# An attention kernel with image-prompt tokens: the hand-written order of its units is rearranged

## The chip, the cores and the metric

The kernel runs on one core of a Trainium2 chip. The metric is the device time of one execution in microseconds (us), lower is better. The engines are TensorE (PE in the rows; PEld is its weight load), VectorE (DVE), ScalarE (ACT), GpSimd (POOL) and SyncE (SP, which here only issues transfers).

## What is computed

Eight batches of cross attention with 20 heads of 16 channels. The context has 371 text tokens and 4 image-prompt tokens.

```python
q = heads(x @ W_q); k = heads(text @ W_k); v = heads(text @ W_v)
probs = softmax(q k^T * D**-0.5)                 # 112 x 371, 20 heads, 8 batches
text_out = probs @ v
k_ip, v_ip = heads(ip @ W_k_ip), heads(ip @ W_v_ip)
qsem = l2norm(probs @ text)                      # 112 x 512 for each head
sem  = qsem @ l2norm(ip)^T
p_ip = softmax(q k_ip^T * D**-0.5 + 0.5 * sem) * mask
out  = (text_out + p_ip @ v_ip) @ W_out + b_out + x
```

The norm of `probs @ text` is not formed from its 512 columns. It is e G e^T with the Gram matrix G = text text^T, of which only the upper blocks are used; that is why a diagonal block has to be halved and corrected before it can be multiplied.

## The kernel before

Every engine walks one list of units, `master_schedule()`, and issues what that unit means for it; a unit that means nothing to an engine is skipped. So the list sets the program order of all five queues at once, and semaphores do the rest. For VectorE the list is passed through `behind()` (line 142), which holds back a K, G or GV unit until after the next max, gram, mT or o.

A batch b is five rounds (groups of four heads), g = 5b + r. The words of a round stand in `ROUNDS` for batches 1 to 6, `EARLY` for batch 0, `LATE` for the last round of batches 5 and 6, `SECOND` and `NO_K` for the first round of batches 1 and 6, and `LAST` for batch 7. While batch b is worked on, batch n = b + 1 is prepared and batch b + 2 gets its keys. The words that matter here:

- `S0 S1 S2` (St): scores of round g + 1 in three blocks of keys. Four matmuls of 99 rows into P (line 1276), then two ScalarE passes, exp into `eb` and a rounded copy into `er` (lines 813, 817). S0 of a batch's first round waits for the rows of maxima, `s_mr` (line 1273).
- `g2 g1 g0` (gram, lines 1279 to 1295): Gram block column times `er`, 5, 3 and 1 matmuls into Y. VectorE multiplies the product by `eb` (line 1025), GpSimd adds the products of g1 and g0 (line 633).
- `v` (pv): values and row sums of the previous round into O (line 1309).
- `m` (max): scores of one head of batch n, without exp, and their row maximum on VectorE (line 1001). All 20 come before `mT`, which transposes them; SP then writes three rows into `qst` (line 519).
- `K0 K1 K2`: keys of batch b + 2, from `eh` and `el`, the rounded and the rest part of the context. `Kr`: SP loads them back in stacked form (lines 494 to 514).
- `E` (split): for batch b + 3, ScalarE makes the two halves of `eh` (line 739), then GpSimd the two halves of `el` (line 644).
- `C`, `G0 G1 GV V0 V1`: Gram blocks and values of batch n.
- `D`: VectorE's three steps on the diagonal blocks of n: `dl` (line 974), `lh` (line 978), and `Gh` times a triangle (line 980). `L`: a matmul with `dl` (line 1229) and VectorE's five steps after it (lines 989, 994, 997); the first g2 of batch n waits for the last, `s_wd` (line 1286).
- `p`, `pT`, `cT`, `o`: end of batch b - 1. ScalarE evicts pT into `pTs` (line 851); cT (lines 1343 to 1354) needs that and gives `cTh` on ScalarE and `cTl` on VectorE (line 1101); `o` is nine matmuls that need `cTl` (line 1391).
- `T0 T1 r0 r1 r2 pw z`: the small steps of batch b - 1's image-prompt softmax.

The units with results in the three banks `PR` share them in turn (`seq`, `NR`), so a unit waits until the third before it has been read.

Of the kernel before, what the change touches and what calls it, by code (L numbers as in the profile page):

```python
# [5 lines left out]
B, S, C, E = 8, 112, 320, 512  # L6
NTOK, NIP = 375, 4
T = NTOK - NIP
H, D = 20, 16
# [17 lines left out]
K0 = (len(STACK) + 6) * 16  # L27
# [9 lines left out]
def spread(core, *others):  # L37

    keyed = []
    for w, units in enumerate((core,) + others):  # L40
        keyed += [((k + 0.5) / len(units), w, u) for k, u in enumerate(units)]
    return [u for _, _, u in sorted(keyed, key=lambda t: (t[0], t[1]))]


def flat(units):
# [2 lines left out]

ROUNDS = ("K0 S0 m g2 m g1 S1 m K1 m S2 m g0 v G0",
# [4 lines left out]
SECOND = "S0 K0 m g2 g1 m S1 m g0 K1 m v S2 m G0"  # L56
NO_K = "m m S0 g2 m g1 v g0 S1 S2 m m G0"
EARLY = ("m S1- m S2- K1 S0 m g2 g1 S1 m m g0 m S2 K2",
# [4 lines left out]
LATE = "p g2 pT g1 S0 g0 D cT S1 L S2 v o"  # L63
LAST = ("S0 S1 v g2 S2 g1 T0 T1 g0",
# [4 lines left out]

# [1 line left out]
def master_schedule():  # L71

    def split(b):  # L80
        return [("E", b, 0), ("El", b, 0), ("E", b, 1), ("El", b, 1)]

    qs = [[("q", c, n) for c in range(3)] for n in range(2)]
    order = [("wq",), ("wk", 0), ("wkl", 0)] + split(0) + [("wk", 1), ("wkl", 1), ("wk2",)] + qs[0][:1] + [("xq",)] + qs[0][1:]
    order += [("K", 0, c) for c in range(3)] + [("Kr", 0), ("w", 1)] + qs[1] + [("kip", c) for c in range(3)] + [("vip",)]
    order += [("G", 0, 0)] + split(1)[:2] + [("G", 0, 1)] + split(1)[2:] + [("G", 0, 2)] + [("K", 1, c) for c in range(3)] + [("Kr", 1)]
    order += [("D", 0)]
    side = [("V", 0, 1), ("L", 0), ("V", 0, 2)] + [("qip", b) for b in range(B)]
    side = [("V", 0, 0)] + spread(side[:-1], [("max", 0, h) for h in range(H)]) + side[-1:]
    cut = side.index(("qip", 3))  # L90
    order += side[:cut] + split(2) + side[cut:]
    order += [("mT", 0)] + [("G", 1, i) for i in range(2)] + [("K", 2, 0), ("V", 1, 0), ("V", 1, 1), ("St", 0, 0)]
    for b in range(B):
        n, f = b + 1, b - 1
        maxes = iter([("max", n, h) for h in range(H)])
        for r, words in enumerate(LAST if n == B else ROUNDS if b else EARLY):
            g = NG * b + r
            unit = {"S0": ("St", g + 1, 0), "S1": ("St", g + 1, 1), "S2": ("St", g + 1, 2)} if g + 1 < NG * B else {}
            if g:
                unit.update({"v": ("pv", g - 1)})  # L100
            if n < B:
                unit.update({"V0": ("V", n, 0), "V1": ("V", n, 1), "GV": ("GV", n), "C": ("C", n), "mT": ("mT", n)})
                unit.update({"D": ("D", n), "L": ("L", n)})
            if b and n < B:
                unit.update({"G0": ("G", n, 0), "G1": ("G", n, 1), })
            if n + 1 < B:
                unit.update({"K0": ("K", n + 1, 0), "K1": ("K", n + 1, 1), "K2": ("K", n + 1, 2), "Kr": ("Kr", n + 1)})
            if b:
                unit.update({"T0": ("T", f, 0), "T1": ("T", f, 1), "pw": ("pw", f, 0), "pv": ("pw", f, 1), "r0": ("r", f, 0, 0), "r1": ("r", f, 0, 1),
                             "r2": ("r", f, 0, 2), "z": ("z", f, 0), "p": ("p", f, 0), "pT": ("pT", f), "cT": ("cT", f),  # L110
                             "o": ("o", f)})
            if n == B:
                unit.update({"vW": ("vW", b)})
                unit.update({"T0'": ("T", b, 0), "T1'": ("T", b, 1), "pw'": ("pw", b, 0), "pv'": ("pw", b, 1), "r0'": ("r", b, 0, 0), "r1'": ("r", b, 0, 1),
                             "r2'": ("r", b, 0, 2), "z'": ("z", b, 0), "p'": ("p", b, 0)})
            if b == 0:
                unit.update({"wo": ("wo",), "S1-": ("St", g, 1), "S2-": ("St", g, 2)})
            if b in (B - 3, B - 2) and r == NG - 1:
                words = LATE
            if b == 1 and r == 0:  # L120
                words = SECOND
            if b == B - 2 and r == 0:
                words = NO_K
            for w in words.split():
                if w == "g":
                    order += [("gram", g, j) for j in (2, 1, 0)]
                elif w in ("g2", "g1", "g0"):
                    order.append(("gram", g, int(w[1])))
                elif w == "m":
                    order += [u for u in [next(maxes, None)] if u and n < B]  # L130
                elif w == "E":
                    order += split(b + 3) if b + 3 < B else []
                elif w in unit:
                    order.append(unit[w])
    b = B - 1
    order += [("pv", NG * B - 1), ("z", b, 0), ("T", b, 2), ("p", b, 0), ("end", 0), ("cT0", b), ("vWo", b, 0), ("pw", b, 2)]
    order += [("vWo", b, 1), ("cT", b), ("o", b - 1), ("ot", b, 0), ("end", 1), ("z", b, 1), ("cTl", b), ("ot", b, 1), ("end", 2)]
    order += [("sum", b - 1), ("pT", b), ("ot", b, 2), ("o", b)]
    return order
# [43 lines left out]
def build(nc, xT, xr, ctxT, ctxip, mask, wq, wk, wv, wkip, wvip, wout, bout, ident_d, tri_d, hm_q, hm_v, krow, out):  # L183
    f32, bf16 = mybir.dt.float32, mybir.dt.bfloat16
    ALU = mybir.AluOpType
    ACT = mybir.ActivationFunctionType
    AX = mybir.AxisListType
    order = master_schedule()
    seq = {u: n for n, u in enumerate([u for u in order if u[0] in RING])}
    posp = {u: n for n, u in enumerate([u for u in order if u[0] in PRO])}  # L190
# [1252 lines left out]
```

## Time and profile before

| | before |
|---|---|
| median of three runs | 390.13 us (387.19 to 395.4) |
| profiled execution | 389.0 us |
| its span, first to last instruction | 387.0 us |
| TensorE busy | 358.2 us, mean granted clock 0.974 |
| VectorE, ScalarE, GpSimd busy | 269.1, 215.7, 213.1 us |

The span is what the rows below are measured in. A row of the timeline gives start, duration, engine, line of the kernel, operation, tiles and shapes, and in brackets how long the engine had been idle before it and what ended that wait. TensorE's matmuls overlap, so their durations sum to more than the time between their starts.

### The profile page before, as it was taken

Reading aid. Unit: us, or ns where it says so; the run is one execution under the profiler, and the core shown is the slowest. Engines: PE = TensorE matmul, PEld = TensorE weight load, DVE = VectorE, ACT = ScalarE, POOL = GpSimd, SP = SyncE. Lnnn points to the kernel's source line nnn. Section 1 sums busy time; section 2 is a strip of 40 time slices with the busy share of each in tenths; the row PEclk is TensorE's granted clock in tenths of the full one; section 3 lists DMA queues with packets and bytes.
Section 4 is the critical chain, followed back from the end, with each engine's and each line's share of the span. In section 5 each row is a group of like instructions: output and inputs, shape, how many; then the busy total and the mean of one; then the engine's idle time right before and its main releaser. Section 6 shows DMA issues by size and latency. Waiting matters only on the chain.

```text
span 387.0 us, 9366 instructions
## 1 busy us (share of the span) xinstructions
PE 358.2 (93%) x3498; PEld 304.9 (79%) x3498; DVE 269.1 (70%) x566; ACT 215.7 (56%) x490; POOL 213.1 (55%) x230
## 2 busy tenths in 40 slices
PE   8999799995899979999899979998999899999886
PEld 7879599874788868888788878886888678877664
DVE  4897673693667695587858685687758587867464
ACT  6734133783557455647556554757455458557741
POOL 8020271397138861596438662696349615865872
PEclk9999999998799989999999989999999999999899
DMA  8999993259105802265205702283203710002001
GB/s 265 313 240 188 249 188 105 64 169 157 23 1 158 155 13 59 81 142 103 75 5 176 134 22 65 82 179 63 77 3 103 128 42 3 2 3 58 0 3 31
DMA packets 30145, 38.01 MB, mean 98 GB/s; under 512 B 14394, under 2 KB 27307, under 8 KB 29419
## 3 DMA queue, kind: packets, MB, share of 16 engines
q1 hardware_dynamic: 29732, 37.00, 41.1%
q8 instruction: 28, 0.46, 0.5%
q10 hardware_dynamic: 368, 0.41, 0.3%
q14 instruction: 17, 0.14, 0.1%
HBM read 28.49 MB, written 8.81 MB: 96 GB/s over the span
## 4 chain that ended last, share of the span: by engine, by line
PE 64%; DVE 16%; DMA 9%; issue 6%; SPq 3%; ACT 1%; POOL 0%; DVEq 0%; ACTq 0%
PE PR L1127 32%; PE Y L1127 18%; PE O L1127 7%; PE P L1127 5%; DVE mx L1001 4%; DMA qst<-ma 3%; DVE dl L974 3%; DMA tri<-tri_d 2%; DMA big<-xT 2%; DVE pb L1025 2%; DVE ssq L885 1%; DMA kd<-ks 1%; PE PR L1326 1%; DVE cTl L1101 1%; SPq L519 1%
## 5 line engine op out<-in xcount | busy, mean ns | idle before, releaser
L633 POOL TENSOR_TENSOR pb<-pb 128x448 f32<-128x448 f32 x78 | 91.2, 1170 | 99.9 <-DVE pb L1025 96.9
L1001 DVE TENSOR_REDUCE mx<-PR 112x1 f32<-112x371 f32 x160 | 81.6, 536 | 50.5 <-PE PR L1127 49.5
L1025 DVE TENSOR_TENSOR pb<-big,Y 128x448 f32<-128x448 f32 x120 | 73.5, 617 | 32.1 <-PE Y L1127 30.5
L813 ACT ACTIVATE big<-P 128x448 f32<-128x448 f32 x120 | 64.7, 539 | 55.0 <-PE P L1127 55.0
L1127 PE MATMUL Y<-er,Gh 128*128 128x448 f32 x240 | 93.4, 413 | 1.7 <-ACT er L817 1.4
L817 ACT ACTIVATE er<-big 128x448 fp32r<-128x448 f32 x120 | 69.4, 578 | 3.8
L1127 PE MATMUL P<-qst,kst 99*128 99x112 bf16 x480 | 44.0, 218 | 9.4 <-DMA qst<-ma 9.0
L1127 PEld LDWEIGHTS Y<-er,Gh 128*128 128x128 f32 x240 | 46.1, 192 | 8.0 <-issue 2.3
L1127 PE MATMUL PR<-kst,qst 96*112 96x371 bf16 x160 | 48.7, 329 | 2.5 <-DVE mx L1001 2.1
L1127 PEld LDWEIGHTS P<-qst,kst 99*128 99x128 bf16 x480 | 30.6, 101 | 25.1 <-issue 17.8
L1127 PE MATMUL Y<-er,Gl 128*128 128x448 f32 x120 | 44.4, 370 | 0.0
L1127 PE MATMUL PR<-wvh,eh 128*128 128x320 f32 (+2 forms) x96 | 32.9, 342 | 0.8 <-DVE Gl L989 0.8
L1127 PE MATMUL O<-big,Vt 128*23 128x112 f32 x960 | 31.5, 265 | 0.0
L1127 PE MATMUL PR<-wvh,el 128*128 128x320 f32 (+2 forms) x96 | 31.5, 328 | 0.0
L1127 PE MATMUL PR<-wvl,eh 128*128 128x320 f32 (+2 forms) x96 | 31.4, 327 | 0.0
L664 POOL TENSOR_TENSOR t<-ssq,halfm 112x20 f32<-112x20 f32 (+3 forms) x11 | 29.6, 2687 | 1.6 <-DVE ssq L885 1.6
L644 POOL TENSOR_TENSOR el<-et,eh 128x752 fp32r<-128x752 f32 x12 | 22.4, 1890 | 9.3 <-ACT eh L739 9.3
L1127 PEld LDWEIGHTS O<-big,Vt 128*23 128x23 f32 x960 | 21.4, 103 | 7.3 <-issue 5.7
L1127 PEld LDWEIGHTS PR<-kst,qst 96*112 96x112 bf16 x160 | 19.5, 130 | 7.4 <-DVE mx L1001 5.2
L1127 PEld LDWEIGHTS Y<-er,Gl 128*128 128x128 f32 x120 | 23.0, 192 | 1.1
L1127 PE MATMUL PR<-eh,wkh 128*128 128x372 f32 x64 | 22.9, 358 | 0.0
L1127 PE MATMUL PR<-eh 128*128 128x376 f32 (+2 forms) x68 | 21.9, 322 | 0.0
(208 smaller groups left out, 719.1 us busy)
## 6 DMA issues: line engine op xcount, KB each, us to landing
et<-ctxT SPq DMA_DIRECT2D x7, 752.0 KB, 4.9
kst<-kd SPq DMA_DIRECT2D x7, 720.0 KB, 7.4
kd<-ks SPq DMA_DIRECT2D x16, 288.0 KB, 2.9
qst<-qd SPq DMA_DIRECT2D x48, 70.0 KB, 3.5
kst<-kd SPq DMA_DIRECT2D x7, 480.0 KB, 9.5
kst<-kd SPq DMA_DIRECT2D x9, 240.0 KB, 9.1
qd<-kst SPq DMA_DIRECT2D x4, 336.0 KB, 7.8
vx<-xr SPq DMA_DIRECT2D x8, 140.0 KB, 2.5
```

The source lines that it names most:

```text
L519: sp.dma_start(qst[b % 3][96 + j:97 + j, :, :], ma[:, j, :]).then_inc(s_mr[b % 2], 16)
L633: pool.tensor_tensor(total, total, (pz, pm)[j], ALU.add).then_inc(s_S, 1)
L644: pool.tensor_tensor(el[b % 2][:, sl, :], et[:, sl, :], eh[b % 2][:, sl, :].bitcast(f32), ALU.subtract).then_inc(s_el, 1)
L664: power = pool.tensor_tensor(t1[:, hs], ssq[:, hs], halfm[:, hs], ALU.pow)
L813: act.activation(e, P[(3 * g + c) % 2][:, 0:448], ACT.Exp).then_inc(s_exp, 1)
L817: act.activation(er[g % 2][:, 448 * c:448 * c + 448], e, ACT.Copy).then_inc(s_er, 1)
L885: dve.scalar_tensor_tensor(ssq[:, hs], t1[:, hs], EPS * EPS, lq[:, hs], ALU.mult, ALU.max).then_inc(s_clamp, 1)
L974: dve.scalar_tensor_tensor(dl[:, :, :], Gl[b % 2][:, :, 0:128].bitcast(f32), 0.5, ident[:, :].unsqueeze(1).broadcast_to([128, 3, 128]), AL ...
L1001: dve.tensor_reduce(mx[b % 2][:, h:h + 1], bank[0:S, 0:T], AX.X, ALU.max).then_inc(s_free[seq[u] % NR], 1)
L1025: dve.tensor_tensor((pz, pm, pa[g % 2])[j], eb[g % 3][:, 448 * j:448 * j + 448], Y[y % 2][:, 0:448], ALU.mult).then_inc(s_P, 1)
L1101: dve.tensor_tensor(lo[:, c:3, :], bank[:, c * S:3 * S].rearrange("p (c s) -> p c s", c=3 - c), hi[:, c:3, :].bitcast(f32), ALU.subtract). ...
L1127: return pe.matmul(o, st, mv, start=start, stop=stop, **kw)
```

## The change

Only the words of the rounds and one line of the prologue's order change. No unit is added or removed, and no instruction changes its shape; units change places, and with them the turn in which the `PR` banks are used.

```diff
--- before.py
+++ after.py
@@ -48,22 +48,22 @@
 
 
 
-ROUNDS = ("K0 S0 m g2 m g1 S1 m K1 m S2 m g0 v G0",
-          "S0 m g2 g1 m S1 m g0 K2 C v m S2 G1 m",
-          "S0 m g2 T0 T1 g1 m g0 r0 S1 m pw S2 m v V0 m",
-          "Kr r1 m g2 g1 S0 m m g0 V1 S1 m m S2 v r2 mT z GV",
-          "p g2 pT E g1 D cT S0 S1 v g0 L o S2")
-SECOND = "S0 K0 m g2 g1 m S1 m g0 K1 m v S2 m G0"
-NO_K = "m m S0 g2 m g1 v g0 S1 S2 m m G0"
-EARLY = ("m S1- m S2- K1 S0 m g2 g1 S1 m m g0 m S2 K2",
-         "S0 m g2 g1 S1 m g0 S2 m v m m wo C",
-         "S0 m g2 g1 m S1 g0 m m S2 v m",
-         "Kr S0 m S1 m g2 m g1 m v g0 S2 mT GV",
-         "E g2 g1 S0 g0 D v S1 S2 L")
-LATE = "p g2 pT g1 S0 g0 D cT S1 L S2 v o"
-LAST = ("S0 S1 v g2 S2 g1 T0 T1 g0",
+ROUNDS = ("K0 S0 m g2 m g1 m K1 S1 S2 m m g0 v G0",
+          "g2 S0 m g1 m g0 S1 m v K2 C m S2 G1 m",
+          "Kr S0 m g2 T0 m T1 g1 g0 S1 r0 m pw S2 m v V0",
+          "m r1 g2 g1 S0 m m g0 V1 m S1 m S2 m v r2 mT z GV",
+          "p g2 g1 pT E D cT S0 S1 v S2 L o g0")
+SECOND = "K0 S0 m g2 g1 m S1 m g0 K1 m v S2 m G0"
+NO_K = "m m S0 g2 m g1 S1 v g0 S2 m G0 m"
+EARLY = ("m S1- m S2- K1 S0 S1 m g2 g1 m m S2 g0 K2 m",
+         "m g2 S0 g1 S1 m g0 S2 m v m m wo C",
+         "Kr S0 m g2 g1 m S1 g0 m m S2 v m",
+         "S0 m S1 m g2 m g1 m v g0 S2 mT GV D",
+         "E g2 g1 v S0 g0 S1 S2 L")
+LATE = "p g2 pT D g1 g0 cT S0 S1 L S2 v o"
+LAST = ("S0 v S1 g2 S2 g1 T0 T1 g0",
         "S0 r0 g2 g1 pw v S1 g0 pv S2",
-        "S0 r1 g2 S1 r2 g1 g0 S2 v",
+        "r1 S0 g2 S1 g1 r2 g0 S2 v",
         "S0 g2 S1 z g1 p g0 S2 v",
         "pT T0' pw' r0' g2 cT g1 g0 r1' v vW T1' r2' pv'")
 
@@ -84,8 +84,7 @@
     order = [("wq",), ("wk", 0), ("wkl", 0)] + split(0) + [("wk", 1), ("wkl", 1), ("wk2",)] + qs[0][:1] + [("xq",)] + qs[0][1:]
     order += [("K", 0, c) for c in range(3)] + [("Kr", 0), ("w", 1)] + qs[1] + [("kip", c) for c in range(3)] + [("vip",)]
     order += [("G", 0, 0)] + split(1)[:2] + [("G", 0, 1)] + split(1)[2:] + [("G", 0, 2)] + [("K", 1, c) for c in range(3)] + [("Kr", 1)]
-    order += [("D", 0)]
-    side = [("V", 0, 1), ("L", 0), ("V", 0, 2)] + [("qip", b) for b in range(B)]
+    side = [("V", 0, 1), ("D", 0), ("V", 0, 2), ("L", 0)] + [("qip", b) for b in range(B)]
     side = [("V", 0, 0)] + spread(side[:-1], [("max", 0, h) for h in range(H)]) + side[-1:]
     cut = side.index(("qip", 3))
     order += side[:cut] + split(2) + side[cut:]
```

What each queue sees of it, read off the two lists:

- SP: its stream is the same. Nothing that SP acts on lies between the old place of `Kr` (start of the fourth round) and the new (start of the third).
- GpSimd: in batches 1 to 4 the sum of the last round's g1 (line 633) now stands before the two `el` halves of `E`, where it stood behind them; in batch 7 one such sum stands before `r2`. All else is the same.
- VectorE: in the prologue `D` of batch 0 stands behind the third maximum instead of before the first, and `L` behind the sixth instead of the third. In batches 1 to 4 the last round has `L` and `o` before g0 instead of behind it; in batch 0 (for batch 1) `D` comes before g2, g1 and g0, and in batches 5 and 6 before g1 and g0. Elsewhere maxima and products trade places by one or two.
- ScalarE: blocks of scores trade places with K, v and L.
- TensorE: the last round of batches 1 to 4 goes from g2 pT g1 cT S0 S1 v g0 L o S2 to g2 g1 pT cT S0 S1 v S2 L o g0; that of batches 5 and 6 from g2 pT g1 S0 g0 cT S1 L S2 v o to g2 pT g1 g0 cT S0 S1 L S2 v o; in batch 0, v goes ahead of S0. In the other rounds S, m, g and K trade places with their neighbours.

## Rows read from the trace of the kernel before

**Rows 1.** Page, part 1: busy time, share, instructions of TensorE and weight load

```profile
PE 358.2 (93%) x3498; PEld 304.9 (79%) x3498; DVE 269.1 (70%) x566; ACT 215.7 (56%) x490; POOL 213.1 (55%) x230
```

**Rows 2.** Waits: who waited for whom; total us, times, longest

```profile
PE P L1127 <- DMA qst<-ma: 9.0, 5, 5.3
...
PE PR L1127 <- DVE cTl L1101: 7.3, 6, 2.1
```

**Rows 3.** Timeline, TensorE in the prologue: a maximum, and the third V

```profile
43.65 0.36 PE L1127 MATMUL PR<-kst,qst 96*112 96x371 bf16 x1 [1.87 <-DVE mx L1001]
...
45.79 0.40 PE L1127 MATMUL PR<-wvh,eh 128*115 128x320 f32 x1 [0.77 <-DVE Gl L989]
```

**Rows 4.** Timeline, VectorE in the prologue: diagonal steps, then maxima

```profile
41.53 0.56 DVE L974 SCALAR_TENSOR_TENSOR dl<-Gl,ident 128x384 fp32r<-128x384 f32 x1 [3.03 <-DMA tri<-tri_d]
...
51.25 5.95 DVE L1001 TENSOR_REDUCE mx<-PR 112x1 f32<-112x371 f32 x13 [0.60 <-PE PR L1127]
```

**Rows 5.** Timeline, TensorE: its waits at the last rounds of batches 0 to 5

```profile
97.79 0.53 PE L1127 MATMUL P<-qst,kst 99*128 99x112 bf16 x4 [5.35 <-DMA qst<-ma]
...
142.10 0.43 PE L1127 MATMUL PR<-woh,cTh 128*112 128x320 f32 x1 [1.95 <-DVE cTl L1101]
...
182.18 0.55 PE L1127 MATMUL P<-qst,kst 99*128 99x112 bf16 x8 [0.48 <-DMA qst<-ma]
...
185.61 0.38 PE L1127 MATMUL PR<-woh,cTh 128*112 128x320 f32 x1 [1.41 <-DVE cTl L1101]
...
227.62 0.58 PE L1127 MATMUL PR<-woh,cTh 128*112 128x320 f32 x1 [2.06 <-DVE cTl L1101]
...
309.93 0.36 PE L1127 MATMUL P<-qst,kst 99*128 99x112 bf16 x4 [2.15 <-DMA qst<-ma]
```

**Rows 6.** Timeline, VectorE in the last rounds of batches 3 and 5

```profile
222.90 2.08 DVE L974 SCALAR_TENSOR_TENSOR dl<-Gl,ident 128x384 fp32r<-128x384 f32 x1
...
225.48 1.57 DVE L980 TENSOR_TENSOR Gh<-Gh,tri 128x384 fp32r<-128x384 f32 x1
226.97 0.49 DVE L1101 TENSOR_TENSOR cTl<-PR,cTh 128x336 fp32r<-128x336 f32 x1
...
229.79 0.56 DVE L997 TENSOR_TENSOR Gh<-Gh,Gl 128x384 fp32r<-128x384 f32 x1
...
311.12 0.55 DVE L974 SCALAR_TENSOR_TENSOR dl<-Gl,ident 128x384 fp32r<-128x384 f32 x1
...
312.18 0.91 DVE L980 TENSOR_TENSOR Gh<-Gh,tri 128x384 fp32r<-128x384 f32 x1
```

**Rows 7.** Timeline, GpSimd in the same two rounds

```profile
222.78 3.85 POOL L644 TENSOR_TENSOR el<-et,eh 128x752 fp32r<-128x752 f32 x2 [1.75 <-ACT eh L739]
...
311.28 1.39 POOL L633 TENSOR_TENSOR pb<-pb 128x448 f32<-128x448 f32 x1 [1.64 <-DVE pb L1025]
```

**Rows 8.** Windows of 4 us behind three of the waits: busy time, granted clock (PEclk)

```profile
142.00:146.00 4.00, 3.90 (x18) 3.70 (x19) 3.16 (x7) 0.86 (x2) 1.68 (x2) 0.57 0.01 4
228.00:232.00 4.00, 4.00 (x20) 3.77 (x20) 2.77 (x6) 1.12 (x2) 1.19 (x2) 0.62 0.05 13
...
185.00:189.00 4.00, 3.39 (x24) 3.30 (x25) 3.68 (x9) 1.27 (x3) 2.19 (x2) 1.00 0.00 0
```

**Rows 9.** Timeline, TensorE: pT, the first matmuls of cT, S0 with S1

```profile
221.43 0.26 PE L1331 MATMUL PR<-ident,pe_ 112*80 112x112 f32 x1
...
222.16 0.42 PE L1127 MATMUL PR<-ident,tn 112*128 112x112 f32 x2
...
223.53 0.56 PE L1127 MATMUL P<-qst,kst 99*128 99x112 bf16 x8
```

**Rows 10.** Timeline, ScalarE: the eviction of pT in batch 3

```profile
221.72 0.26 ACT L851 ACTIVATE pTs<-PR 80x112 f32<-80x112 f32 x1 [0.38 <-PE PR L1331]
```

**Rows 11.** Chain that ended last, in order of time: v behind a wait, and elsewhere

```profile
98.82 1.64 PE O L1127 x32
...
194.81 0.90 PE O L1127 x32
```

## The prediction, made before the changed kernel ran

> **What bounds the kernel now.** I read the page first: TensorE is busy in 93% of the span, no other engine in more than 70% [rows 1]. The work of TensorE is the same after the change, so the change can only move what TensorE waits for, and its clock. I then listed who waits for whom, and every idle stretch of TensorE in its timeline. Idle are 28.8 us, 387.0 less 358.2. The large stretches come at one place, the last round of a batch: 9.0 us in five waits of S0 for the rows of maxima and 7.3 us in six waits of `o` for `cTl` [rows 2]. One by one they are 5.35 us in batch 0; 1.95 in batch 1; 0.48 and 1.41 in batch 2; 2.06 in batch 3; 2.15 in batch 5 [rows 5]; what the two totals leave, 1.0 and 1.9 us, is in batches 4 to 6. The prologue has 1.87 and 0.77 us [rows 3]. Behind the two waits of about 2 us the granted clock was 0.57 and 0.62 for 4 us, behind that of 1.41 it was 1.00 [rows 8]; 1.00 is 2.4 GHz, and the lower level 1.2.
>
> Why is `cTl` late? On VectorE it stands behind `D`. In batch 3 `dl` took 2.08 us and the triangle step 1.57; in batch 5, which has no `el`, the same instructions took 0.55 and 0.91 [rows 6]. GpSimd ran the two `el` halves from 222.78 to 226.63, over both slow ones [rows 7]. `dl` ended between the halves and the triangle step 0.4 us behind the second. So a VectorE step with both operands in SBUF waits for the GpSimd instruction that is running, and slips in at its end.
>
> **Part 1, `el` behind the sum of g1, batches 1 to 4.** I replay batch 3 with durations of rows. VectorE does g2, GV and g1 as before and starts `dl` at 222.90. GpSimd now starts with the sum of g1, which in batch 5 started during `dl` and took 1.39 us, as it had to wait itself [rows 7]. So `dl` ends at 223.45, `lh` (0.55, as the gap between `dl` and the triangle step in batch 5 shows) at 224.0, and the triangle step takes 0.91 as in batch 5 and ends near 224.9 [rows 6]. `cTl` (0.49) ends near 225.4, in place of 227.46: 2.1 us sooner.
>
> TensorE meets it later than before. g1 now stands before pT, which used to cover pT's eviction: pT started at 221.43, ScalarE's eviction at 221.72 took 0.26, and cT followed at 222.16 behind g1 [rows 9, 10]. Now pT is at 222.05 and cT can start at about 222.65: a new wait of 0.5 us. Then cT takes 1.4 and S0 with S1 0.5 [rows 9], v 0.9 [rows 11], and S2 and the matmul of `L` 0.4: `o` is reached near 225.85, behind `cTl`. Its wait is gone. Moved work: S2 goes ahead and g0 behind, the same sum. S2 needs the exp of S0, one ScalarE pass behind `cTh`; by the eviction rows that is ready near 225.3, as TensorE gets there. S0 comes 0.5 us later, so its waits of 0.48 us and the like go too.
>
> Per batch that returns the wait and costs 0.5. Sum over the four batches: 1.95 + 1.41 + 2.06 + about 1.4 (of the 1.9 left) = 6.8, the waits of S0 in batches 2 and 4, 0.48 and, as half of the 1.0 left, 0.45, so 0.9, less 2.0: 5.7 us. The clock adds to it. Work at 0.57 and 0.62 over 4 us loses 1.7 and 1.5 us [rows 8], and I see no idle stretch left that is as long as those before it: 3.2 us. Part 1 is **8.9 us**. If the new wait is nothing it is 10.9; if it is 1.0 us it is 6.9; if the clock falls anyway, 5.7.
>
> What is late next: the `el` halves, each (3.85 - 0.3)/2 = 1.78 us, now run from 224.9 to about 228.4 [rows 7]. Two things are behind them. K0 needs the second half at its third group, near 228.5 by my count, so with no slack to speak of. And VectorE's last two `L` steps have both operands in SBUF; they meet the second half and end near 229.4 (229.79 + 0.56 before), while g2 of the next batch is reached near 229.9 [rows 6]. Both are hidden by 0.1 to 0.5 us; if not, each tenth costs 0.4 us over the four. I take 0 and keep 2 us for the range.
>
> The Trainium skill bears on this place ("SBUF — State Buffer", section "SBUF: two separate sides"): VectorE and GpSimd share a pair of ports as an exclusive lock, and whichever starts first holds it for the whole instruction. The rows agree as far as one instruction goes (2.08 in place of 0.55 us). By that rule the change moves a collision rather than removing it, from `D` to `L`; it is the third rival below.
>
> **Part 2, the last rounds of batches 5 and 6.** g0 and cT (0.2 + 1.4 us) now stand before S0, so they run while the rows of maxima travel. In batch 5 the wait of 2.15 shrinks to about 0.6 [rows 5]; in batch 6 the wait goes. With `D` before g1, `cTl` is ready in time. Gain 1.6 + 0.8 = **2.4 us**; 0 if the rows of maxima come later by as much.
>
> **Part 3, batch 0.** v ahead of S0 puts 0.9 us of work into the wait of 5.35 [rows 5, 11]. Behind the wait, at the low clock, it took 1.64; the low stretch then covers other work, so I count **0.9 us**. The wait itself stays: what SP issues is unchanged, so the keys of batch 2 are loaded neither sooner nor later. Moving `Kr` is worth nothing.
>
> **Part 4, the prologue.** `D` waited 3.03 us for its triangle to land, and the maxima waited behind it [rows 4]. Now three maxima go first, the first as soon as it is there, the next two from 41.75 at 0.458 each (13 in 5.95) [rows 4]: 42.7. `D` takes three times 0.55 with overlap, 44.2; three more maxima 45.6; `L` 2.3 (in batch 3, 230.35 less 227.46 less a product of 0.6 [rows 6]), 47.9; two maxima 48.85; the last twelve without a gap 54.5. Before, the last ended at 57.2 [rows 4]. TensorE alternates maxima with small products at the same pace, and the third V no longer waits [rows 3]. Gain 2.7; I take **2.5 us**, as all later work follows from these maxima. The bounds are 1 us (if the `el` halves for K of batch 2, behind a long GpSimd step, hold the end) and 3.
>
> **Part 5, the rest.** In the other rounds S, m, g and K trade places where TensorE has no wait of 0.15 us or more in its timeline; nothing can be gained there. A bank read too late could cost: bounds 0 and 2 us, I take 0, since each unit moves by one or two places and the banks' readers with it. In batch 7 one sum stands before `r2`: 0, bounds 0.5 either way.
>
> **Sum.** 8.9 + 2.4 + 0.9 + 2.5 = 14.7 us. The profiled execution took 389.0 with a span of 387.0; that gives a span of 372.3 and a time of 374.3. The median shown is 1.1 above the profiled execution, and the runs spread over 8 us, so I say **374.8**.
>
> **Rivals.** 1. *The gain is smaller, the waits move.* Each last round gets a new wait (pT's eviction, S2's exp, the second `el` half) of 1 us more than I count, in six rounds: 6 us back, and with a clock that falls twice 9: 381 to 384. For it: the replay has three places with less than 0.5 us to spare. Against: each is counted from a row. 2. *Nothing changes.* SP's stream is unchanged, and if the rows of maxima set the pace of every batch, TensorE meets them at the same moment: only 0 to 3 us go, 387 to 390. Against: in batches 1 and 3 S0 did not wait at all, and `o` did. 3. *Slower.* The lock starves GpSimd: it gets its ports only behind all of VectorE's `D`, `cTl` and `L` steps, so that the second `el` half ends at 233 instead of 228.4. K0 then waits 4.5 us and the clock falls for 4 us (1.7) in four batches: 25 us on top of the forecast, 399. It decides from 15/4 = 3.7 us of lateness per batch. Against: `cTl` and three `L` steps read a PSUM bank, and the one that ran beside the sums kept its 0.49 us [rows 6].
>
> **How the numbers follow.** Forecast 0.77, rival 1 0.16, rival 2 0.04, rival 3 0.03. The forecast's own range: 370.5 (new wait nothing, prologue 3, and up to 1 more) to 380 (prologue 1, clock falls, 2 us at `el`). To hold 8 in 10 I add the near half of rival 1: 370.5 to 381.5. Over 2% faster, about what a measurement of this kernel can tell from no change, is under 382.3: all of the forecast and nearly half of rival 1, 0.84; within 2% 0.13; slower 0.03.
>
> **What would show it.** In the profile after: `dl` near 0.55 and the triangle step near 0.9 us in batches 1 to 4; no wait of `o` for `cTl` over 0.3; a new wait of cT of about 0.5; the clock at 1.00 through the last rounds of batches 1 and 3; the wait of batch 0 at 4.4 to 4.6 and that of batch 5 near 0.6; the last maximum of the prologue near 54.5. Wrong would be a wait of K0 for `el`, or of g2 for the `L` steps, over 0.5 us.

## The result: faster by 4.1%, in the forecast range

| | before | after |
|---|---|---|
| median | 389.68 us (4 runs, 387.19 to 395.4) | 372.78 us (4 runs, 372.23 to 374.11) |
| profiled execution, its span | 389.0, 387.0 us | 374.1, 372.1 us |
| TensorE busy, mean granted clock | 358.2 us, 0.974 | 353.5 us, 0.991 |
| TensorE idle in the span | 28.8 us | 18.6 us |

The ratio is 0.9592, with a 95% interval of 0.9536 to 0.9648. The forecast was 374.8 in 370.5 to 381.5. For the profiled execution by itself it was 374.3, and it took 374.1. Of the 14.9 us that its span lost, 10.2 are idle time of TensorE and 4.7 are busy time of the same 3498 matmuls. Most of the 4.7 goes with the clock, as more of them ran at the full one; 1.3 of it does not (see the table below).

The engines of the kernel after, part 1 of its page (busy us, share, instructions); to be read against [rows 1]:

```profile
PE 353.5 (95%) x3498; PEld 302.5 (81%) x3498; DVE 266.1 (72%) x566; ACT 214.5 (58%) x490; POOL 212.9 (57%) x230
```

What TensorE waited for, after (us in total, times, longest); against [rows 2]:

```profile
PE P L1126 <- DMA qst<-ma: 6.0, 3, 4.9
PE PR L1126 <- ACT pTs L850: 1.9, 4, 0.6
PE Y L1126 <- POOL Gh L556: 1.5, 1, 1.5
PE Y L1126 <- ACT er L816: 1.4, 1, 1.4
PE P L1126 <- ACT big L812: 0.9, 4, 0.3
PE PR L1126 <- DVE mx L1000: 0.9, 1, 0.9
```

The line of `o` for `cTl`, 7.3 us in six waits before, is gone. In its place stand four waits of cT for ScalarE's eviction of pT, 1.9 in all. The waits for the rows of maxima fell from 9.0 to 6.0. (One line of the file went, so a line of after has a number one lower.)

The last round before batch 4 is prepared, after. First VectorE (start, us, tiles, idle time before); against [rows 6]:

```profile
216.33 0.55 DVE L973 SCALAR_TENSOR_TENSOR dl<-Gl,ident 128x384 fp32r<-128x384 f32 x1
216.91 0.55 DVE L977 TENSOR_REDUCE lh<-dl 128x3 f32<-128x384 f32 x1
217.38 0.91 DVE L979 TENSOR_TENSOR Gh<-Gh,tri 128x384 fp32r<-128x384 f32 x1
218.26 0.51 DVE L1100 TENSOR_TENSOR cTl<-PR,cTh 128x336 fp32r<-128x336 f32 x1
219.64 1.22 DVE L988 SCALAR_TENSOR_TENSOR Gl<-Gl,lh,PR 128x371 fp32r<-128x371 f32 x3 [0.87 <-PE PR L1126]
220.90 1.25 DVE L993 TENSOR_TENSOR Gl<-Gl,tri 128x384 fp32r<-128x384 f32 x1
222.18 0.56 DVE L996 TENSOR_TENSOR Gh<-Gh,Gl 128x384 fp32r<-128x384 f32 x1
```

GpSimd in the same stretch; against [rows 7]:

```profile
216.49 1.39 POOL L632 TENSOR_TENSOR pb<-pb 128x448 f32<-128x448 f32 x1 [1.79 <-DVE pb L1024]
217.84 3.89 POOL L643 TENSOR_TENSOR el<-et,eh 128x752 fp32r<-128x752 f32 x2
```

And TensorE:

```profile
216.18 0.45 PE L1126 MATMUL PR<-ident,tn 112*128 112x112 f32 x2 [0.44 <-ACT pTs L850]
...
219.44 0.31 PE L1126 MATMUL PR<-woh,cTh 128*112 128x320 f32 x1
...
222.16 0.33 PE L1126 MATMUL PR<-el,wkh 128*128 128x372 f32 x1
...
223.25 0.50 PE L1126 MATMUL Y<-er,Gh 128*128 128x448 f32 x1
```

`dl` takes 0.55 us and the triangle step 0.91, as counted, because GpSimd now runs the sum beside them (216.49 to 217.88) and starts `el` at 217.84, half a microsecond into the triangle step. (The 0.91 still holds a wait for the end of the sum: in the prologue, after, with no sum beside it, the same step took 0.55.) `cTl` ends at 218.77 and `o` starts at 219.44 without a wait. The collision didn't vanish: the triangle step of `L` (220.90) has both operands in SBUF, meets the second `el` half and takes 1.25 us in place of 0.56. It hurts nobody, as the first g2 of the next batch comes at 223.25, 0.5 us behind the end of `L`, and the K0 matmul that reads the last piece of `el` comes 0.4 us behind the end of `el` (221.73). That is the lock which the Trainium skill describes ("SBUF — State Buffer", section "SBUF: two separate sides"): whichever of the two engines starts first has the shared ports for its whole instruction, and the other waits. The rows agree for instructions with two SBUF operands; `cTl`, which reads a PSUM bank, kept its 0.51 us beside a running `el`.

Where the 14.9 us went, by the start of `mT` in each batch (the last rounds of batches 1 to 4 lie in the stretches up to batches 3 to 6):

| stretch, up to | before | after | gained | forecast |
|---|---|---|---|---|
| `mT` of batch 0 (prologue) | 57.34 | 55.55 | 1.8 | 2.5 |
| batch 1 | 88.17 | 85.93 | 0.4 | 0 |
| batch 2 (holds batch 0's last round) | 132.32 | 130.49 | −0.4 | 0.9 |
| batches 3 to 6 | 303.27 | 291.35 | 10.1 | 8.9 |
| batch 7 | 340.48 | 326.83 | 1.7 | 1.6 |
| end | 387.0 | 372.1 | 1.3 | 0.8 |

In batches 3 to 6 TensorE's idle time fell by 5.8 us (5.7 forecast) and its busy time by 4.3. Of these 4.3, 3.0 belong to the two slow stretches behind the waits of 1.95 and 2.06 us, which are gone (3.2 forecast). The other 1.3 were saved at the full clock: 40.0 us of busy time per batch before, 39.6 to 39.7 after.

The profile of before has five stretches at half the clock, and the prediction priced two of them. One more lies in the wait of batch 0, which comes below; one in the prologue, from 46.7 to 50.1 us; and one near the end, right behind a wait of only 1.37 us for `er`. The kernel after has the same wait of 1.37 us, at the full clock behind it. The two windows behind that wait, before and after (0.50 and 1.00 are the granted clock):

```profile
360.70:364.10 3.40, 3.40 (x13) 2.57 (x12) 0.62 (x1) 1.78 (x4) 3.32 (x3) 0.50 0.00 0
```

```profile
346.70:350.10 3.40, 3.40 (x49) 2.55 (x49) 1.77 (x3) 2.67 (x6) 3.32 (x3) 1.00 0.00 0
```

So 0.9 of the last row's 1.3 us is busy time of TensorE, and no change of the order is seen to bring that: in seven of the fourteen profiles the clock fell behind this wait, with the old order and with the new.

### The profile page after: what moved, and what is told of

Same layout as the page of the kernel before. It is cut to its first block, busy times and chain, and to the rows that moved or that the text cites. A ratio compares the mean times of both kernels' runs of the same rounds, so it can differ in the third digit from the quotient of the medians.

```text
span 372.1 us, 9366 instructions
## 1 busy us (share of the span) xinstructions
PE 353.5 (95%) x3498; PEld 302.5 (81%) x3498; DVE 266.1 (72%) x566; ACT 214.5 (58%) x490; POOL 212.9 (57%) x230
## 4 chain that ended last, share of the span: by engine, by line
PE 85%; DVE 5%; DMA 4%; POOL 2%; issue 1%; ACT 1%; SPq 1%; DVEq 0%; POOLq 0%; ACTq 0%
PE PR L1126 43%; PE Y L1126 21%; PE P L1126 10%; PE O L1126 9%; DMA qst<-ma 4%; PE PR L1325 1%; DVE mx L1000 1%; POOL t L663 1%; POOL pb L632 1%; SPq L518 1%; DVE pb L1024 1%; DVE lq L882 0%; PE PR L1261 0%; ACT big L812 0%; DVE pe_ L1076 0%
## 5 line engine op out<-in xcount | busy, mean ns | idle before, releaser
L1024 DVE TENSOR_TENSOR pb<-big,Y 128x448 f32<-128x448 f32 x120 | 72.6, 615 | 33.3 <-PE Y L1126 30.1
L1126 PE MATMUL Y<-er,Gh 128*128 128x448 f32 x240 | 91.7, 406 | 1.6 <-ACT er L816 1.4
L1126 PE MATMUL P<-qst,kst 99*128 99x112 bf16 x480 | 42.8, 217 | 7.0 <-DMA qst<-ma 6.0
L1126 PEld LDWEIGHTS P<-qst,kst 99*128 99x128 bf16 x480 | 29.8, 100 | 21.8 <-issue 14.8
L760 ACT ACTIVATE ks<-PR 128x372 bf16<-128x372 f32 (+1 forms) x24 | 10.3, 428 | 33.8 <-PE PR L1126 33.7
L1126 PEld LDWEIGHTS PR<-kst,qst 96*112 96x112 bf16 x160 | 19.7, 129 | 5.3 <-issue 2.1
```

Of the source, the lines that this page charges most:

```text
L760: act.activation(ks[:, 0, TP * c:TP * c + w], bank[:, 0:w], ACT.Copy).then_inc(s_kh, 1)
L1024: dve.tensor_tensor((pz, pm, pa[g % 2])[j], eb[g % 3][:, 448 * j:448 * j + 448], Y[y % 2][:, 0:448], ALU.mult).then_inc(s_P, 1)
L1126: return pe.matmul(o, st, mv, start=start, stop=stop, **kw)
```

## The experiments

Each kernel was timed beside the kernel before on one chip. a1 to a4 and b3 are the kernel before with one part of the change; the ones below "after" are the kernel after with one part taken back or something added.

| kernel | median us (runs) | ratio to before, 95% | span, clock of its profile |
|---|---|---|---|
| a1_pool | 382.19 (4) | 0.9764 [0.9690, 0.9838] | 378.6, 0.986 |
| a2_last | 382.00 (4) | 0.9734 [0.9671, 0.9798] | 381.1, 0.977 |
| a3_late | 388.53 (10) | 0.9886 [0.9847, 0.9924] | 384.2, 0.971 |
| a4_pro | 389.20 (8) | 0.9957 [0.9911, 1.0002] | 388.7, 0.974 |
| b3_rest | 389.61 (10) | 0.9947 [0.9900, 0.9994] | 385.2, 0.977 |
| after | 372.78 (4) | 0.9592 [0.9536, 0.9648] | 372.1, 0.991 |
| b1_pool_back | 372.76 (4) | 0.9520 [0.9458, 0.9581] | 370.8, 0.989 |
| b2_v_back | 373.09 (4) | 0.9529 [0.9467, 0.9591] | 372.3, 0.991 |
| c1_pT | 373.66 (4) | 0.9548 [0.9468, 0.9629] | 371.5, 0.991 |
| d1_el_back | 382.61 (4) | 0.9787 [0.9744, 0.9831] | 380.9, 0.976 |
| b4_hold | 372.00 (4) | 0.9526 [0.9473, 0.9579] | 369.5, 0.988 |
| d5_wo | 371.69 (4) | 0.9509 [0.9466, 0.9553] | 370.3, 0.995 |
| d4_keys | 370.35 (4) | 0.9484 [0.9429, 0.9539] | 367.6, 1.000 |

The kernel before had medians of 391.57, 391.39 and 391.12 in the three sittings (a; b and c; d with b4), so ratios compare better across them than microseconds do. The kernel after was timed in a sitting of its own, where before had 389.68; it was not timed again beside the kernels made from it. Its ratio of 0.9592 and b1_pool_back's of 0.9520 have nearly the same microseconds behind them, so a difference of 1 or 2 us between after and one of these kernels is not settled by such a number alone.

### The parts alone, on top of before

**a1_pool**: only GpSimd's order changes; in batches 1 to 4 the sum of g1 goes ahead of the two `el` halves.

```diff
+def pool_order(order, sum_first):
+    for b in range(1, B - 3):
+        u = ("gram", NG * b + NG - 1, 1)
+        ...  # u moves ahead of ("El", b + 3, 0), or behind ("El", b + 3, 1)
-            for u in order:
+            for u in pool_order(order, True):
```

> Before, with one thing of the change: in the last rounds of batches 1 to 4 GpSimd adds the product of g1 ahead of the two el halves; all other engines' streams are as before. Theory (port lock): dl falls from 2.08 to 0.55 us and the triangle step from 1.57 to 0.91, cTl comes 2.1 us sooner, TensorE's waits of o for cTl in batches 1 to 4 (6.9 us) go and with them the low clock behind two of them (3.2 us): 10 us less, 379 in place of 389. A wait of K0 for the second el half may give back 0.2 us a batch. Rival (TensorE's order, S2 ahead of o and g0 behind, is what hides the wait): at most 3 us less.

**a2_last**: only the last round of batches 1 to 4.

```diff
-          "p g2 pT E g1 D cT S0 S1 v g0 L o S2")
+          "p g2 g1 pT E D cT S0 S1 v S2 L o g0")
```

> Before, with the last round of batches 1 to 4 written as in the change (all engines) and nothing else. Theory: as the run with GpSimd's order alone, less 0.5 us in each of four batches for the new wait of cT for pT's eviction, plus the waits of S0 in batches 2 and 4 (0.9 us): 9 to 10 us less. If TensorE's order mattered by itself, this run would be several us better than the one with GpSimd's order alone.

By the medians both give the same: 9.4 us for one change of place on GpSimd, 9.6 us for the whole round, with intervals of 6 to 12 and 8 to 13. So nearly all of the gain of Part 1 comes from taking `el` out of VectorE's way. Whether the order on TensorE adds a little the medians can't tell. In the profiles the stretches up to batches 3 to 6 lost 8.3 us in a1_pool and 9.7 in a2_last, with the same idle time and the full clock in both; the difference is busy time, 40.1 us per batch against 39.7. That is where most of the 1.3 us at the full clock belong. In a1_pool `o` has no wait for `cTl` in batches 1 to 4, and in a2_last cT has its four waits of 0.44 to 0.55.

**a3_late** and **a4_pro**: only `LATE`, and only the prologue's order.

```diff
-LATE = "p g2 pT g1 S0 g0 D cT S1 L S2 v o"
+LATE = "p g2 pT D g1 g0 cT S0 S1 L S2 v o"
```

> Before, with only the last rounds of batches 5 and 6 as in the change (g0 and cT ahead of S0, D ahead of g1). Theory: 2.4 us less, S0's wait in batch 5 from 2.15 to 0.6 us and in batch 6 from 0.55 to 0. Rival (the rows of maxima are a fixed distance behind whatever TensorE does): 0.

```diff
-    order += [("D", 0)]
-    side = [("V", 0, 1), ("L", 0), ("V", 0, 2)] + [("qip", b) for b in range(B)]
+    side = [("V", 0, 1), ("D", 0), ("V", 0, 2), ("L", 0)] + [("qip", b) for b in range(B)]
```

> Before, with only the prologue's part of the change (D behind three maxima, L behind six). Theory: the last maximum comes 1.8 us sooner, as in the changed kernel, and nothing later takes it back: 1.8 us less. Rival: the wait for the rows of maxima in batch 0 (5.35 us), which ends with the transfers, takes it back: 0, with that wait near 7 us.

a3_late gained 3.0 us by the medians (3 to 6 by the interval). In its profile S0 waited for the rows of maxima 0.56 us in batch 5 and not at all in batch 6, in place of 2.15 and 0.55: that bears out the 2.4 us of Part 2. a4_pro is inconclusive on its size. Its `mT` of batch 0 starts at 55.45, 1.9 us sooner than before, as in the kernel after; but its span is 388.7, no shorter, because the clock fell behind three of its waits for `cTl` (1.94, 2.05 and 1.82 us), and for 6.8 us at the wait of batch 5, while in the profile of before it fell behind two and not there. Its median is 2.4 us lower, with an interval that just holds no change.

**b3_rest**: the other rounds (`ROUNDS[0..3]`, `SECOND`, `NO_K`, `LAST`), nothing else.

> The changed kernel without its prologue, its EARLY rounds and the last rounds of batches 1 to 6: what is left is the order of the other rounds, SECOND, NO_K and LAST. Forecast: 0 against before (389), bounds 2 us slower and 0.5 faster. Rival: these moves carry part of the 15 us, since the parts seen one by one in the trace of after sum to 0.5 to 1.5 more per batch than I counted in batches 4 and 6: 2 to 3 us faster.

About 2 us (0.5%), with an interval that barely leaves out zero. I had this part at 0, with bounds from a loss. In its profile, 1.8 us shorter than that of before, most of the gain is the clock's: in the stretches up to batches 3 to 6, which lost 1.7 us, it fell once and not twice, though a wait of 2.04 us for `cTl` was there again. TensorE's busy time per batch at the full clock was 39.7 to 39.9 in place of 40.0.

### The parts taken back, from after

**b1_pool_back**: the reverse of a1_pool in the kernel after, `el` ahead of the sum of g1 on GpSimd (`pool_order(order, False)`).

> The changed kernel, with one thing undone: in the last rounds of batches 1 to 4 GpSimd does the two el halves ahead of the sum of g1 again. In the changed kernel pT stands behind g1, so the eh halves are ready about 0.9 us later than before. Theory by replay of its trace: dl (216.33) starts before the first el half (eh ready at 216.8), the triangle step waits for that half until 218.65 and cTl ends near 219.6 in place of 218.8, while o is reached at 219.44: a wait of 0.2 us a batch, 1 us in all, 374. Rival (the order on GpSimd is needed whatever the rest): 7 to 10 us more, 380 to 383.

Nothing was lost, though my account of Part 1 had its gain hang on this order. VectorE's rows in it, last round of batch 3:

```profile
214.23 0.55 DVE L984 SCALAR_TENSOR_TENSOR dl<-Gl,ident 128x384 fp32r<-128x384 f32 x1
214.82 0.55 DVE L988 TENSOR_REDUCE lh<-dl 128x3 f32<-128x384 f32 x1
215.29 1.65 DVE L990 TENSOR_TENSOR Gh<-Gh,tri 128x384 fp32r<-128x384 f32 x1
216.86 0.49 DVE L1111 TENSOR_TENSOR cTl<-PR,cTh 128x336 fp32r<-128x336 f32 x1
```

and GpSimd's:

```profile
214.73 3.88 POOL L654 TENSOR_TENSOR el<-et,eh 128x752 fp32r<-128x752 f32 x2 [2.13 <-ACT eh L749]
```

`el` starts half a microsecond behind `dl` although nothing stands ahead of it: it waited 2.13 us for `eh`, its source, which ScalarE makes behind the eviction of pT. Since pT now stands behind g1, that is later too. One step is still slow (1.65), but `cTl` ends at 217.35 and `o` starts at 217.50, with no wait for it of 0.2 us or more. This is about what I expected of the run, and my rival for it, that GpSimd's order is needed whatever the rest, is out.

**d1_el_back** takes both away: `E` stays behind pT, pT goes back ahead of g1, and `el` ahead of the sum.

```diff
-          "p g2 g1 pT E D cT S0 S1 v S2 L o g0")
+          "p g2 pT E g1 D cT S0 S1 v S2 L o g0")
```

> The changed kernel with both things that keep the el halves off dl undone in batches 1 to 4: pT back ahead of g1 (so that eh is ready early) and the el halves ahead of the sum of g1 (p g2 pT E g1 D cT ...). TensorE's other moves there, S2 ahead of L and o and g0 behind them, stay. Theory (the collision on VectorE is the whole of it): dl near 2.08 and the triangle step near 1.57 us again, waits of o for cTl of 1.4 to 2.1 us in four batches and the low clock behind two or more of them: 8 to 12 us more than the changed kernel, 381 to 385. Rival (either TensorE's order or the other rounds hide it): less than 4 us more.

This one tells it: 382.61 us, 9.8 more than after's median and 10.6 more than b4_hold, timed in the same sitting (by the ratios to before, 7.6 more than after), though TensorE keeps S2 ahead of and g0 behind `o`. VectorE, last round of batch 3:

```profile
219.93 2.09 DVE L973 SCALAR_TENSOR_TENSOR dl<-Gl,ident 128x384 fp32r<-128x384 f32 x1
222.06 0.55 DVE L977 TENSOR_REDUCE lh<-dl 128x3 f32<-128x384 f32 x1
222.53 1.56 DVE L979 TENSOR_TENSOR Gh<-Gh,tri 128x384 fp32r<-128x384 f32 x1
224.01 0.49 DVE L1100 TENSOR_TENSOR cTl<-PR,cTh 128x336 fp32r<-128x336 f32 x1
```

and TensorE's waits:

```profile
PE PR L1126 <- DVE cTl L1100: 7.0, 4, 2.1
PE P L1126 <- DMA qst<-ma: 6.1, 3, 4.4
```

The durations of before (2.08 and 1.57) are back, and with them the waits of `o`: 7.0 us in four.

**c1_pT**: pT ahead of g1 again, but `el` still behind the sum. It should return the 1.9 us of cT's waits.

```diff
-          "p g2 g1 pT E D cT S0 S1 v S2 L o g0")
+          "p g2 pT g1 E D cT S0 S1 v S2 L o g0")
```

> The changed kernel with pT of the last rounds of batches 1 to 4 back ahead of g1 (p g2 pT g1 E D cT ...), so that g1 covers pT's eviction again while the el halves stay behind the sum of g1. Theory: cT's wait of 0.44 to 0.55 us goes in four batches, 1.9 us; K0 then comes within 0.3 us of the second el half and may wait 0.2 us a batch: 0.8 to 1.9 us less than the changed kernel, 371 to 372. Rival: the low slack behind the el halves takes all of it back: 373.

It gave 373.66, no gain. cT doesn't wait, but S0, reached sooner, waits for the rows of maxima, 1.04 us in batch 2 and 0.27 in batch 3, and pT waits 0.56 for its input in batch 1. Wherever S0 waited for these rows in batches 1 to 5, it started 6.1 to 7.3 us behind the start of `mT`, over all kernels, and 5.0 to 5.1 in batch 6. This travel is the next bound of the last rounds: time won ahead of S0 is lost at S0.

### The long wait of batch 0

**b2_v_back**: v goes back behind g0 in the last round of batch 0.

```diff
-         "E g2 g1 v S0 g0 S1 S2 L")
+         "E g2 g1 S0 g0 v S1 S2 L")
```

> The changed kernel, with v of batch 0's last round back behind g0 (E g2 g1 S0 g0 v S1 S2 L). Theory of the forecast: 0.9 us more. What the traces suggest instead: v ahead of the wait only moves the low clock later, from 94.5-101.4 us in before to 95.9-102.4 in after, where it lies over work and not over idle time, so that undoing it costs nothing or gains up to 1 us.

373.09 against 372.78, a difference that can't be measured. The profile of after can't settle it either, for it had bad luck here. From `mT` of batch 1 to `mT` of batch 2, the stretch with this wait, the program of all engines is the same in after, b1_pool_back, c1_pT and d1_el_back; it is one and the same, too, in before, a1_pool, a2_last, a3_late and a4_pro. b3_rest has the new rounds of batch 1 and the old last round of batch 0. In us:

| kernel | v | rounds of batch 1 | wait of S0 | stretch | at half the clock, of it over work |
|---|---|---|---|---|---|
| after | ahead | new | 4.93 | 44.6 | 6.8, 6.5 |
| b1_pool_back | ahead | new | 3.82 | 42.4 | 3.4, 3.4 |
| c1_pT | ahead | new | 4.49 | 42.7 | 3.4, 3.4 |
| d1_el_back | ahead | new | 4.39 | 42.8 | 3.4, 3.3 |
| b2_v_back | behind | new | 5.97 | 44.4 | 6.8, 3.1 |
| b3_rest | behind | new | 5.19 | 43.7 | 3.4, 3.4 |
| before | behind | old | 5.35 | 44.1 | 6.8, 3.5 |
| a1_pool | behind | old | 6.23 | 45.2 | 6.8, 4.2 |
| a2_last | behind | old | 6.03 | 45.7 | 6.8, 5.8 |
| a3_late | behind | old | 5.28 | 44.1 | 6.8, 3.5 |
| a4_pro | behind | old | 5.17 | 44.0 | 3.4, 3.3 |

Between the four kernels with v ahead, the wait and the clock make the difference. After, one row for each microsecond (PE, PEld, DVE, ACT and POOL busy with their instructions, granted clock, share of DMA, GB/s):

```profile
95.00:96.00 1.00, 0.00 (x0) 0.00 (x0) 0.00 (x0) 0.00 (x0) 0.19 (x1) 0.88 0.68 117
96.00:97.00 1.00, 0.92 (x6) 0.69 (x7) 0.00 (x0) 0.34 (x1) 0.00 (x0) 0.50 0.19 49
...
101.00:102.00 1.00, 1.00 (x6) 0.71 (x5) 0.00 (x0) 0.00 (x0) 0.00 (x0) 0.50 0.00 0
102.00:103.00 1.00, 1.00 (x9) 0.97 (x8) 0.22 (x1) 0.92 (x2) 0.00 (x0) 0.70 0.00 0
```

The same view of b1_pool_back:

```profile
96.00:97.00 1.00, 0.84 (x7) 0.82 (x7) 0.47 (x1) 0.97 (x3) 0.45 (x1) 0.64 0.09 31
97.00:98.00 1.00, 1.00 (x5) 1.00 (x4) 0.83 (x2) 0.97 (x3) 0.69 (x1) 0.50 0.00 0
98.00:99.00 1.00, 1.00 (x5) 1.00 (x4) 0.95 (x3) 0.97 (x3) 0.00 (x0) 0.50 0.00 0
99.00:100.00 1.00, 1.00 (x5) 1.00 (x5) 0.56 (x1) 0.04 (x1) 0.00 (x0) 0.66 0.00 0
```

The kernel after stood at half the clock (1.2 GHz) for 6.8 us, 6.5 of them over work; b1_pool_back for 3.4 us, all over work. Of the 2.2 us between their stretches, 1.2 are busy time of TensorE, the price of 3.1 us more of slow work, and 1.0 is idle time. With the short slow stretch and the same rounds of batch 1, v ahead of S0 gains 0.9 to 1.3 us (42.4 to 42.8 against 43.7, where `D` too has its old place); with the long one it gains nothing (44.6 against 44.4), since the slow stretch then covers work in after and idle time in b2_v_back. The medians put the difference at 0.3. What decides which of the two an execution gets, no run here settles.

The wait itself belongs to transfers. The rows of maxima stand on SP's queue behind the keys of batch 2. Three kernels change when these, or what stands behind the rows, are moved: **b4_hold** has SP wait until batch 1's rows have landed before it issues what stands behind them; **d5_wo** loads the output weights at the start of batch 0; **d4_keys** does that and makes the keys of batch 2 two places sooner.

```diff
+                    if b == 1:
+                        sp.wait_ge(s_mr[1], 48)
                     sp.dma_start(vr[b % 2], vd[b].unsqueeze(0)
```

> The changed kernel, in which SP issues the transfers behind the rows of maxima of batch 1 (values of batch 1, rest of x, queries of batch 3, 0.66 MB) only when those rows have landed. What sets the wait of S0 in batch 0 (3.8 to 6.0 us in the runs so far)? Theory: the keys of batch 2, 1.4 MB issued ahead of the rows, are served first, and what is issued later doesn't matter: the wait stays at 4 to 6 us, 373. Rival (the later transfers share the engines with the rows): the wait falls below 3 us, 370 to 371.

```diff
-EARLY = ("m S1- m S2- K1 S0 S1 m g2 g1 m m S2 g0 K2 m",
-         "m g2 S0 g1 S1 m g0 S2 m v m m wo C",
+EARLY = ("wo m S1- m S2- K1 S0 S1 m g2 g1 m m S2 g0 K2 m",
+         "m g2 S0 g1 S1 m g0 S2 m v m m C",
```

> The changed kernel with the split of W_out (wo) at the start of batch 0 and not in its second round, so that the keys of batch 2, whose loads wait for it, start as soon as they have been written: near 80.5 and not at 81.7 us. Theory (the rows of maxima queue behind these loads): the wait of S0 in batch 0 falls by about 1.2 us: 371.5. Rival: unchanged, 373.

```diff
-EARLY = ("m S1- m S2- K1 S0 S1 m g2 g1 m m S2 g0 K2 m",
+EARLY = ("wo m S1- K1 m S2- K2 S0 S1 m g2 g1 m m S2 g0 m",
```

> The changed kernel with wo at the start of batch 0 and the keys of batch 2 (K1, K2) worked out 2 to 4 us sooner, ahead of the scores of round 1. Their write and their loads start about 4 us sooner, near 77 us. Theory: the loads are over when the rows of maxima come, S0's wait of 3.8 to 6.0 us in batch 0 falls to about 1 us, and with no long idle stretch the low clock behind it (6.5 us at 0.5, 3.2 us of work) goes too: 6 to 8 us less, 365 to 367. Rival (the rows need 6 to 7 us from mT whatever else is loaded, as in the other batches, and mT follows K): the wait stays at 2 us or more and the clock still falls: 370.

The wait was 3.46 us in b4_hold, between the 4 to 6 of my theory and the under 3 of its rival, 2.81 in d5_wo, and in d4_keys:

```profile
93.59 0.36 PE L1126 MATMUL P<-qst,kst 99*128 99x112 bf16 x4 [1.78 <-DMA qst<-ma]
```

d4_keys is the fastest kernel of all, 370.35 us (369.62 to 371.27), below every run of after, and 1.3 to 1.7 us below the medians of d5_wo and b4_hold, timed in the same sitting. Its clock was 1.000 in two of four runs. The gain of 2.4 us is a third of the 6 to 8 I expected. The load of the keys was issued only 1.2 us sooner (80.44 against 81.66; SP had another load ahead of it), `mT` of batch 1 came 0.6 us later, and waits of 0.2 to 0.7 us appeared. In its profile the clock did not fall at all, and the stretch up to `mT` of batch 2 took 39.7 us, against 42.4 to 44.6 with after's order. The runs of b4_hold (371.20 to 374.04) and d5_wo (370.92 to 372.32) overlap with those of after, so what each does to the time isn't shown. That transfers make the wait long is shown as far as this: it was 3.8 to 4.9 us in the four kernels with after's order, and 3.46, 2.81 and 1.78, one profile each, with other orders of SP's work.

### The clock, run by run

The mean granted clock is known for every run. The 36 executions of the kernel before beside these experiments (one that took 1172 us is left out) ran from 386.8 to 396.1 us, at clocks of 0.982 down to 0.951. A straight line through them gives 2.4 us for each 0.01 of clock, with a correlation of −0.91, and leaves 0.9 us unexplained; through the 26 below 392.5 us it gives 1.9, with −0.84. So most of the 9 us over which the kernel before spreads goes with the clock.

The profiles show where it falls. Of the twelve waits of `o` for `cTl` from 1.8 to 2.1 us, in before, a3, a4, b3 and d1, nine had the half clock behind them; in d1_el_back those of 1.97 and 2.06, but not that of 2.07. The waits for `cTl` of 1.1 to 1.4 us had none. But length alone doesn't decide it, for the wait of 1.37 us for `er` in batch 7, the same in all fourteen profiles, had the half clock behind it in seven. That these cases of chance make the spread of before is argued only; d1_el_back has such waits too, and its four runs lie within 1.0 us. The four runs of after have 0.985 to 0.995 and spread over 2 us, and there the clock does not order them: 372.8 us at 0.985, 374.1 at 0.991. From a mean of 0.968 to one of 0.990, 4 to 5 of the 17 us would be the clock's; that is an estimate from the two lines, drawn out beyond the clocks they were fitted to.

## Why the prediction was right

**Reading of the bound: right.** Work stayed the same, the waits at the last rounds went.

**Part 1, 8.9 us: right in mechanism, 10.1 measured** in batches 3 to 6 (the table), which holds what Part 5 brings there too; 9.4 to 9.8 by the medians of three experiments. The steps of the replay held within 0.1 us: `dl` 0.55, triangle step 0.91, cT's new wait 0.44 to 0.55 in place of 0.5, `o` without a wait. Only `el` started 0.5 us sooner than counted, and its pair took 3.89 us where I had counted 3.6, so that it ended when I said. Idle time (5.8 for 5.7) and clock (3.0 for 3.2) came out as counted. The excess of 1.2 is busy time at the full clock, 1.3 us, for which I had no term; it appears with TensorE's order in the last round (a2_last) and not with GpSimd's alone (a1_pool), and why it does stays open. One thing in it was wrong: I put the gain down to the sum going ahead of `el` alone. Moving pT behind g1 delays `el` as well (b1_pool_back), and in the kernel after either is enough: c1_pT and b1_pool_back, with one of the two, lost nothing that can be measured, d1_el_back, with neither, 9.8 us.

**What is late next: right.** The margins were named as 0.1 to 0.5 us, and they came out at 0.5 (`L` to g2) and 0.4 (`el` to K0), costing nothing. The third rival, GpSimd starved by the lock, did not appear: the `el` pair took 3.89 us, 3.85 before.

**Part 2, 2.4 us: right.** Batch 5's wait for the rows went from 2.15 to 0.70, batch 6's went, and a3_late alone gave 3.0 us. The table's last row has 1.3 us for 0.8 because the clock fell near the end in the profile of before and not in that of after, which is luck.

**Part 3, 0.9 us: not confirmed.** In the profiled execution the stretch grew by 0.4 us, by the medians the part brings 0.3, and from one execution to the next it may be worth 0.9 to 1.3, as counted, or nothing. The step that fails in it is "the low stretch then covers other work, so I count 0.9": it took the slow stretch as one of fixed place and length, while the same program had 3.4 us of it or 6.8, and it fell on idle time or on work.

**Part 4, 2.5 us: 1.8.** The last maximum ends at 55.4, and I had 54.5. VectorE in the prologue, after:

```profile
42.44 0.99 DVE L1000 TENSOR_REDUCE mx<-PR 112x1 f32<-112x371 f32 x2 [1.38 <-PE PR L1126]
43.35 0.55 DVE L973 SCALAR_TENSOR_TENSOR dl<-Gl,ident 128x384 fp32r<-128x384 f32 x1
...
48.72 0.99 DVE L1000 TENSOR_REDUCE mx<-PR 112x1 f32<-112x371 f32 x2
...
49.72 5.68 DVE L1000 TENSOR_REDUCE mx<-PR 112x1 f32<-112x371 f32 x12
```

The mis-sized term is the first: I had the third maximum end at 42.7, and it ended at 43.43, as VectorE waited 1.38 us for TensorE, which had the products of a V unit ahead of it. Most of that is not the change's doing: the first product of this V unit, with nothing moved ahead of it, started at 38.29 in the profile of after and at 37.67 in that of before. Behind it each step took what was counted within 0.1 us: `D` from 43.35 to 44.9, the twelve last ones 5.68 for 5.65.

Counted from this first product to `mT` of batch 0, the part brought 2.4 us: 19.7 before, and 17.3 in eight of the nine kernels with the new order. But the mechanism accounts for only 1.0 of them. In before, the half clock stood over the prologue's work from 46.7 to 50.1 us, behind the waits of 1.87 and 0.77; a1_pool has the old order without it and took 18.2, d1_el_back the new order with it and took 18.8. So 1.4 us were the clock's, which my count did not name: it fell there in four of the five profiles with the old order and in one of nine with the new.

**Part 5, 0: 1.8 by b3_rest,** by an interval that nearly holds zero, and in its profile mostly by a slow stretch less. I had given it bounds of 0 and a loss of 2; a gain should have been in them. What the order of these rounds brings by itself isn't shown.

**The clock: right where it was priced.** I took it that only the two waits near 2 us let it fall, and priced these. The trace of before had two more slow stretches over work outside batch 0, in the prologue and behind the wait of 1.37 us near the end, and I gave neither a term.

**The sum, 14.7: 14.9.** Parts 1 and 5 together and the end came out higher, parts 3 and 4 lower; that these cancelled is luck. The range was added up loosely: its terms give 371.3 to 381.5 from 374.8, where I wrote 370.5 to 380 for the forecast's own; the result lies in both. The median lies 1.3 us below the profiled execution, where I had added 0.5. That execution is the longest of the four, and its mean clock, 0.991, is above that of two shorter ones, so the mean clock doesn't explain it.

## What to carry over

When a VectorE step with both operands in SBUF takes several times its usual length beside a GpSimd instruction, look at who stands behind the step, and move the start of the GpSimd instruction, by its place in the queue or by the arrival of its source; 2 us of lateness per batch were worth 9 to 10 us over four batches here. Follow the collision to where it goes, and count the spare time there. Where work moves around a long wait, compare medians: one execution of the same program differed from another by 2 us in that stretch. And before a gain is put down to the change, list all stretches at half the clock in the profile of before, not only those behind the waits that the change removes.

## What the hardware showed that I had not expected

- The mean clock goes with the time of an execution of the kernel before: 2.4 us for 0.01 of it. Within the four runs of after it doesn't. The kernels of which the profile has no wait near 2 us outside batch 0 (after, b1, b2, b4, c1, d4 and d5) spread over 1.4 to 3.3 us, where before spreads over 9; d1, which has three, over 1.0.
- A wait of 1.37 us was enough for the clock to fall behind it in seven of fourteen profiles, while waits of 2.04, 2.05, 2.07 and 2.15 us passed without a fall in one each (b3_rest, a3_late, d1_el_back, before).
- The slow stretch that belongs to the long wait of batch 0 lasted 3.4 us in seven of the fourteen profiles, 6.8 in six, and was missing in d4_keys, where the wait was 1.78 us. Four kernels with the same program there had either length.
- VectorE's steps that read one operand from PSUM (0.49 and 0.51 us for `cTl`, 1.22 for `L`'s three) were not slowed beside GpSimd's `el`, while steps with both in SBUF took 0.7 to 1.5 us more. A step with a single operand in SBUF, `lh`, kept its 0.55 beside `el` too (222.06 in d1_el_back).
